# Two of twenty-five additions per step taken from TensorE and given to transfers in SBUF: products 0, 1 and 10, 11 added in pairs

## The reference

```python
x = x + deform(groupnorm(x))       # 32 groups of 8 channels

def deform(x):                     # DCNv4, 3 x 3 taps
    xdw = depthwise3x3(x) + dw_b
    om = xdw @ om_w + om_b         # per pixel and group: 9 taps x (dx, dy, mask)
    value = x @ vp_w + vp_b
    # every tap samples value bilinearly at its shifted place, times its mask
    out = sum_over_taps(mask * bilinear(value, tap + offset))
    return out @ op_w

x = x + binary_conv3x3(groupnorm(x)) * scale + bias     # second layer
```

## Time and profile before

| | us |
|---|---|
| median of 3 runs | 3860.18 (3853.02 to 3861.33) |
| the profiled execution's own time | 3859.76 |
| its span, first to last instruction | 3858.0 |
| PE busy over the span | 3628.5 (94%) |
| DVE busy | 3510.0 (91%) |
| ACT busy | 2286.0 (59%) |
| POOL busy | 565.0 (15%) |

### The profile page before, as it was taken

How to read it: one execution, slowest core, us unless ns; L and a number is a source line. 1 busy time by engine, 2 the same in 40 slices (tenths; PEclk the granted TensorE clock), 3 DMA queues, 4 the chain that set the end, 5 groups by cost and what they waited for, 6 DMA issues and landing times. The chain is left out here.

```text
span 3858.0 us, 90635 instructions
## 1 busy us (share of the span) xinstructions
PE 3628.5 (94%) x37696; PEld 2369.5 (61%) x37696; DVE 3510.0 (91%) x2757; ACT 2286.0 (59%) x4547; POOL 565.0 (15%) x412
## 2 busy tenths in 40 slices
PE   4899999999999999999999999999999999858998
PEld 2566666666666666666666666666666666623333
DVE  4899999999999999999999999989999999948776
ACT  5556665666666665666556666665566666235554
POOL 0011111101111111111111001111111111104444
PEclk9999999999999999999999999999999999979999
DMA  6454565445555555455545555555544554345563
GB/s 177 100 111 102 110 125 132 101 111 116 124 120 109 114 123 115 94 108 127 131 99 119 112 121 114 107 122 131 118 100 97 106 107 94 52 158 199 209 215 147
DMA packets 319939, 470.35 MB, mean 122 GB/s; under 512 B 37244, under 2 KB 242684, under 8 KB 313736
## 3 DMA queue, kind: packets, MB, share of 16 engines
q0 software_dynamic: 94080, 196.11, 28.4%
q1 hardware_dynamic: 224584, 266.07, 23.2%
q10 hardware_dynamic: 832, 2.10, 0.1%
HBM read 262.53 MB, written 67.41 MB: 86 GB/s over the span
## 5 line engine op out<-in xcount | busy, mean ns | idle before, releaser
L1026 DVE TENSOR_TENSOR pv<-val,wsum 128x2048 f32<-128x2048 f32 x800 | 1811.2, 2286 | 21.4 <-ACT xdw L557 14.6
L796 PEld LDWEIGHTS ps_add<-ident,pv 128*128 128x128 f32 x12800 | 1401.2, 142 | 356.0 <-issue 223.7
L796 PE MATMUL ps_add<-ident,pv 128*128 128x128 f32 x12800 | 1527.2, 275 | 70.9 <-DVE pv L1026 62.7
L751 PE MATMUL ps_om<-xdw,omw 128*32 128x256 f32 x13824 | 868.4, 384 | 30.4 <-ACT hat L587 29.4
L585 ACT ACTIVATE hat<-ps_om,omb 128x256 f32<-128x256 f32 x576 | 276.0, 479 | 551.2 <-PE ps_om L751 501.9
L979 DVE TENSOR_TENSOR prod<-hat,mwy 128x1536 f32<-128x1536 f32 (+1 forms) x384 | 526.0, 1397 | 82.9 <-DMA wsum<-prod 61.8
L472 POOL DMA_DIRECT2D wsum<-prod x192 | 226.0, 1254 | 2556.8 <-DVE wsum L979 2556.8
L751 PEld LDWEIGHTS ps_om<-xdw,omw 128*32 128x32 f32 x13824 | 391.2, 109 | 330.2 <-issue 95.5
L589 ACT ACTIVATE msk<-ps_om,omb 128x256 f32<-128x256 f32 x288 | 137.0, 476 | 401.4 <-PE ps_om L751 399.3
L965 DVE TENSOR_TENSOR mwy<-hat,msk 128x768 f32<-128x768 f32 x288 | 274.4, 953 | 94.3 <-ACT hat L599 94.3
L722 PE MATMUL ps_bg<-tri,diag 128*32 128x512 f32 x3024 | 346.5, 592 | 11.9 <-ACT tri L551 11.9
(11 more groups left out here) (134 smaller groups left out, 2622.7 us busy)
## 6 DMA issues: line engine op xcount, KB each, us to landing
wsum<-prod POOLq DMA_DIRECT2D x160, 768.0 KB, 7.1
tri<-in_x_dram SPq DMA_DIRECT2D x725, 128.0 KB, 2.9
win<-in_x_dram SPq DMA_DIRECT2D x144, 256.0 KB, 3.6
x<-xres SPq DMA_DIRECT2D x128, 256.0 KB, 5.1
xres<-in_x_dram POOLq DMA_DIRECT2D x124, 256.0 KB, 8.4
out_dram<-c_x SPq DMA_DIRECT2D x31, 1024.0 KB, 4.5
c_x<-x SPq DMA_DIRECT2D x30, 1024.0 KB, 5.3
c_box<-box_d SPq DMA_DIRECT2D x16, 1024.0 KB, 7.4
```

Of the source, the lines that this page charges most:

```text
L751: mm = nc.tensor.matmul(ps_om[G * q:G * q + G, (par + i) % 2, 0:TOK], omw[:, h, comp, :], xdw[:, j % 2, h, q, :], start=h == 0, stop=h == ...
L796: mm = nc.tensor.matmul(ps_add[:, tb, c, :], pv[:, (j + uv) % PBUF, c, P * tb:P * tb + P], consts["ident"][:, :], start=uv == 0 and c % 4 ...
L1026: nc.vector.tensor_tensor(pv[:, (j + uv) % PBUF, :, :].rearrange("p c (r w) -> p c r w", w=W), val[:, :, SR * j + u:SR * j + u + SR, v:v + ...
```

## The change

Products 0 and 1, and 10 and 11, are added in SBUF by a transfer from POOL's queue that reads the one buffer of `pv` and accumulates into the other (1 MB each), so that PE adds 23 instead of 25. PE adds 1 (which now holds 0 + 1) at the end of slot 5, and 11 (10 + 11) after the depthwise matmuls of slot 0. `pv` has five buffers instead of four. The room comes from `acc`, which now lies in `xres`, and from x ahead, whose two halves go through one buffer one after the other: the first is loaded after slot 7's sends and read by DVE at the end of slot 8, and only then the second is loaded, read in slot 1. ACT's copy of the sums into `acc` now waits for the stores of `xres`, which it did one slot later before. Code and numbers of what is left:

```diff
-PBUF = 4
+PBUF = 5
+PAIRED = {1: 0, 11: 10}
+PAIRS = list(PAIRED)
+ADDS_AT = [(13, 11, 14, 15), (16, 17, 18), (19, 20, 21), (22, 23, 24), (), (2, 3, 1), (4, 5, 6), (7, 8, 9), (12,)]
-        MEANS_AT = [1, 3]
-        SCALES_AT = [0, 2, 4, 6]
+        MEANS_AT = [2, 3]
+        SCALES_AT = [1, 2, 4, 6]
-        AHEAD_AT = 7
+        AHEAD_AT = 8
+                def add_pair(n, j, uv):
+                    s = STEPS * n + j
+                    pool.wait_ge(pv_full, SHIFTS * s + uv + 1)
+                    at_least(pool, pair_added, 16 * (len(PAIRS) * s + PAIRS.index(uv)))
+                    nc.gpsimd.dma_start(pv[:, (SHIFTS * j + uv) % PBUF, :, :], pv[:, (SHIFTS * j + PAIRED[uv]) % PBUF, :, :],
+                                        accum_op=ALU.add).then_inc(pair_added, 16)
...
                 def summed(s):
-                    act.wait_ge(add_done, SHIFTS * (s + 1))
+                    act.wait_ge(add_done, ADDS * (s + 1))
+                    at_least(act, x2_stored, 16 * Q * s)
...
                 def add(s, j, uv):
-                    pe.wait_ge(pv_full, SHIFTS * s + uv + 1)
-                    if uv == 0:
+                    if uv in PAIRED:
+                        pe.wait_ge(pair_added, 16 * (len(PAIRS) * s + PAIRS.index(uv) + 1))
+                    else:
+                        pe.wait_ge(pv_full, SHIFTS * s + uv + 1)
+                    if uv == ADDED[0]:
...
-                    def add_next(k, i):
-                        if k < SAMPLED and not first:
-                            add(s - 1, j - 1, SAMPLES_AT[k][i])
-                        elif k >= SAMPLED and i < len(SAMPLES_AT[k]):
-                            add(s, j, SAMPLES_AT[k][i])
+                    def add_next(k, early):
+                        before = [uv for uv in ADDS_AT[k][:1] if uv not in PAIRED]
+                        for uv in before if early else ADDS_AT[k][len(before):]:
...
-                    if not isinstance(s, int) or s > 0 or uv >= PBUF:
-                        dve.wait_ge(add_done, SHIFTS * s + uv - PBUF + 1)
+                    used, in_step = (uv - PBUF, s) if uv >= PBUF else (uv - PBUF + SHIFTS, s - 1)
+                    if used in PAIRED.values():
+                        dve.wait_ge(pair_added, 16 * (len(PAIRS) * in_step + list(PAIRED.values()).index(used) + 1))
+                    elif not isinstance(s, int) or in_step >= 0:
+                        dve.wait_ge(add_done, ADDS * in_step + ADDED.index(used) + 1)
```

More of the change, by code:

```diff
@@ L39 @@
 SAMPLED = 4
+PAIRED = {1: 0, 11: 10}
+PAIRS = list(PAIRED)
+ADDS_AT = [(13, 11, 14, 15), (16, 17, 18), (19, 20, 21), (22, 23, 24), (), (2, 3, 1), (4, 5, 6), (7, 8, 9), (12,)]
+ADDED = [uv for k in (4, 5, 6, 7, 8, 0, 1, 2, 3) for uv in ADDS_AT[k]]
+ADDS = len(ADDED)
 SENT_TAPS = (1, 2, 3, 6, 7)
@@ L95, in dw @@
         return only(first, "first", shares(FIRST_VALUES, u, DW_UNITS)) + only(not last, "dw", (u,))
-    return dw(0) + only(means, "mean", (0, 0)) + dw(1) + dw(2) + only(means, "mean", (1, 1)) + dw(3) + values(0) + only(not first, "back", range(4)) + values(1) \
+    return dw(0) + dw(1) + only(means, "mean", (0, 0)) + dw(2) + only(means, "mean", (1, 1)) + dw(3) + values(0) + only(not first, "back", range(4)) + values(1) \
         + only(not first, "project", range(4)) + values(2) + values(3)
@@ L217, in layer0 @@
         pv = sb("pv", [P, PBUF, GC, TOK])
-        acc = sb("acc", [P, TB, Q, GC, G])
         acc_t = sb("acc_t", [P, CH, Q * TOK])
-        ahead = [acc[:, :, :, :, :].rearrange("p b q c g -> p (b q c g)"),
-                 acc_t[:, :, :].rearrange("p h t -> p (h t)")]
+        ahead = acc_t[:, :, :].rearrange("p h t -> p (h t)")
         xres = sb("xres", [P, CH, Q, TOK])
+        acc = xres[:, :, :, :].rearrange("p h q t -> p (h q t)")\
+            .rearrange("p (b q c g) -> p b q c g", b=TB, q=Q, c=GC)
         tri = sb("tri", [P, CB, Q, SR, W])
@@ L454, in load_ahead @@
                         pool.wait_ge(bg_full, unit(n, j, "dw3", NI) + 1)
-                    nc.gpsimd.dma_start(ahead[half], src[:, HW // 2 * half:HW // 2 * (half + 1)]).then_inc(x_ahead[half], 16)
+                    if half == 1:
+                        pool.wait_ge(sums_made, CH * CH * n + CH * j + 1)
+                    nc.gpsimd.dma_start(ahead, src[:, HW // 2 * half:HW // 2 * (half + 1)]).then_inc(x_ahead[half], 16)
                 def add_residual(n, j, units):
@@ L836, in step @@
                             offsets(*ahead_of, 1)
-                        add_next(k, 0)
+                        add_next(k, True)
                         if ahead_of:
@@ L862, in _ @@
                 for k in range(SAMPLED):
-                    for uv in SAMPLES_AT[k]:
+                    for uv in ADDS_AT[k]:
                         add(STEPS * NI - 1, STEPS - 1, uv)
@@ L924, in sums_ahead @@
                     for i in range(HW // 1024):
-                        last = nc.vector.bn_stats(bs1[:, j, HW // 1024 * half + i, :], ahead[half][:, 512 * i:512 * i + 512])
+                        last = nc.vector.bn_stats(bs1[:, j, HW // 1024 * half + i, :], ahead[:, 512 * i:512 * i + 512])
                     last.then_inc(sums_made, 1)
@@ L1077, in step @@
                             mask_rows(*following(n, j), 0)
+                        if k == 1 and j in (1, 2) and has_next(n):
+                            sums_ahead(n, j - 1, 1)
+                        if k == SCALES_AT[0] and has_means(n, j, NI):
+                            dve.wait_ge(sums_made, CH * CH * (n + 1))
                         multiply_next(k, 2)
@@ L1096, in _ @@
                         multiply(NI - 1, STEPS - 1, uv)
-                statistics(NI - 1, STEPS - 2)
+                    if k == 0:
+                        statistics(NI - 1, STEPS - 2)
                 at = unit(NI - 1, STEPS - 1, "project3", NI) + 1 + BACK_UNITS
```

31 lines of the change are left out of this document (16 added, 15 removed).

## The result

| | before | changed |
|---|---|---|
| median of the runs, us | 3858.20 | 4041.18 |
| lowest to highest, us | 3853.02 to 3861.33 | 4037.93 to 4045.10 |
| ratio, 95% interval | | 1.0471 (1.0459 to 1.0484) |
| span of the profiled run, us | 3858.0 | 4038.9 |

Predicted were 3960 us and at most 4025. The direction and the mechanism hold; the loss is 183 us instead of 101.

A forecast was written before the change was run, and what follows sets the result against it. Neither PE nor DVE alone was taken as the bound. Per image, 17.2 us of new waits less 8.0 given back net 9.2, 74 us over 8 images; with 27 for the clock, 3960 us, range 3880 to 4025.

The forecast's parts named there:

- What bounds the kernel: Whole steps: neither PE nor DVE alone is the bound; less work on PE gives back at most 6.5 us per image.
- Rival A: PE's load counts and the order costs nothing, since PE reaches slot 8 late enough to find product 12: 3810 us, chance 0.11.
- Slot 8: PE's third component waits for product 12's addition and starts 5.1 us later, delaying ACT and slot 0's third component equally.
- Product 16: DVE waits for the buffer of 11, added late in slot 0: 3.7 us into step 3, 4.1 into step 0.
- the clock's price: PE's clock falls behind new pauses ahead of slot 0's third component: two per image at 1.7 us, 27 us in all.
- about 0.1 each: Product 16's wait into steps 1 and 2, where DVE does x ahead's statistics first and ACT has no edge to clear.
- rival C: PE's clock falls at nearly every new pause, five more per image, 68 us more: 4025 us, chance 0.12.
- Product 6: DVE waits for the addition of 1 at slot 5's end: 6.3 us in step 3, 2.6 in step 0.
- Given back: Per image, DVE regains 6.5 us of waits for weights and buffers, and about 1.5 of 8.0 us of transfer waits.
- Statistics and means moved by a slot: nothing added: DVE's statistics and means of x ahead, done a slot later, were taken to cost no time.
- The transfers of the pairs: Each 1 MB accumulation on POOL's queue takes 10 us, bounds 7.1 and some 16, hidden behind 12 us of cover.
- rival B: Pair transfers take 16 us instead of 10, so products 15 and 5 wait 3 to 4 us per step: 4050, chance 0.07.

The follow-up runs named there:

- fastest kernel: The changed kernel with product 12 added last in slot 8, product 10 made in slot 7, 15 and 18 a slot later, 1 added before 3: 3821.42 us.
- filled pauses: The changed kernel with matmuls of zeros on PE, 14 ahead of product 12's addition and 22 behind slot 0's addition of 13: 3986.53 us.
- later pair: The fastest kernel with the transfer of products 10 and 11 sent when product 12 is written, not when 11 is: 3825.95 us.

## Why the prediction missed, step by step

**What bounds the kernel: right in direction.** DVE's work did not shrink, and PE's saving became idle time. PE's busy time fell by 38.6 us and not by 120: 122 us of additions are gone, and I put the remaining 83 down to matmuls at the lower clock (durations such as 4.43 for 2.73). The fastest kernel bears this out: with the same 23 additions per step and a granted clock of 1.00 from 200 to 3200 us, its PE is busy 3510.6 us, 118 less than before. Rival A, by which the order costs nothing, is out: PE waits for product 12, by 2.9 to 6.2 us, in steps 0, 1 and 2 of each of images 1 to 6.

**Slot 8: the mechanism is shown.** Undoing this one place brings back 161 us. The term was 5.1 us of delay for the third component. In the rows it started 3.3 us ahead of DVE's cut before (1610.97 and 1614.23) and starts 3.4 behind it now (1694.76 and 1691.40): 6.6, of which 1.45 are the addition at half clock.

**Product 16: 8.0 + 3.4 predicted, 15.9 measured. The first step that failed is the clock's price.** The prediction priced two falls per image at 1.7 us each, and left slot 8's pauses to the range. The trace has 42 such pauses in images 1 to 6 (two at each seam into steps 1 to 3, one into step 0), and a fall behind 39 of them, 6.5 per image. By the rows above the first of a seam costs 1.45 us (3.42 for 1.97), the second 2.6 (4.43 for 2.73, and 1.93 for 1.07). With these two sizes the prediction's own count closes. Into step 3 it put product 16 at 18.9 us behind DVE's cut (1633.1 and 1614.2), and the row has 23.0 (1714.44 and 1691.40), later by 4.1, the two falls. Into step 0 it had a wait of 4.1; with one fall that is 6.7, and product 16 waits 6.6 and 6.8 in images 1 and 7, whose first step is not a turn of the loop. At the five turns it waits 1.7 to 2.1, behind 3.8 us in which DVE has already stood idle, and so the mean is 2.75. Into steps 1 and 2, "about 0.1 each" became 2.85 and 4.14. Into step 1 that is the clock: 0.15 is left where the filled pauses take the falls away. Into step 2 they leave the fall at slot 8 and 2.62, so how much of that is the clock stays open.

This is rival C, which I had given 0.12. C's whole clock term is 27 + 68 = 95 us; the filled pauses, which took away 22 of the 39 falls, returned 55.

**Product 6: 8.9 predicted, 5.1 measured** (by step 0.86, 0, 0, 4.25). PE's count from product 16 to product 6 was right: where product 6 waits, it starts 62.8 us behind product 16 in step 3 and 58.9 in step 0, against 63.2 and 59.5. DVE's count of 56.9 was too short, with 58.6 and 58.2 measured. It was read in one step of one image with 1.1 us of transfer waits in it, and the changed kernel has 2.7 and 2.4 there on the mean.

**Given back: the second step that failed.** Masks gave 4.0 of 6.5. The transfer waits were to fall by 1.5 per image and rose by 4.5. The fall came where it was forecast, behind product 16: slot 2's wait went from 1.5 to 0.2. The rise is in slot 8, from 1.7 to 7.4. What had covered the transfer there before were the mask waits of slot 7 (steps 0 and 3) and x ahead's statistics in slot 7 (steps 0 and 1). With both gone, slot 8 waits 1.8, 2.1, 2.4 and 1.2 us where before only step 2 waited 1.7. The kernel without pairs separates them: it keeps its mask waits, and besides step 2's 1.8 it waits in step 1 alone, 2.0 where there was nothing before. So "Statistics and means moved by a slot: nothing added" held for the time of that kernel (3858.90), but not once the mask waits were gone. That a wait given back is a gain needed a look at what is late next, and that was the transfer (7.1 us from issue to landing). Product 10 in slot 7, which covers it, takes 46 us off.

**The turn of the loop: not foreseen.** It is 3.2 us per image, though product 16's wait into step 0 is smaller behind it, and the later pair shows that taking it away need not give time.

**The transfers of the pairs: right.** The page's row of DMA issues, changed kernel (KB, us from issue to landing):

```profile
pv<-pv POOLq DMA_DIRECT2D x64, 1024.0 KB, 7.3
```

Taken were 10, with bounds of 7.1 and 16; DVE never waits for them, so rival B did not occur. The Trainium skill's fit for this path ("DMA: Bandwidth & Descriptors", "Anatomy of one DMA — SWDGE (gpsimd) path"), by which 1 MiB would be an estimated 4.4 us, is still too low, though by less than the row of 8.9 had it. That row was one of two of its size and queue in the trace before: the other one, which loads the other half of x ahead, has 5.2 (`acc<-in_x_dram`), nearer to the page, and the prediction did not weigh it.

**The sum.** Per image 12.6 predicted and 23.7 measured; the difference is product 16 +4.5, transfers +6.0, turn +3.0, masks +2.2, product 6 -3.8, rest -0.9. Times 8, the excess at product 16, which is the clock but for the open part in step 2, is 36 us and would by itself have stayed in the range (3996); the transfers are 48, the turn 24 and the masks 18, less 30 for product 6. So two steps failed: the clock, priced for two falls per image where there are 6.5, and the transfer waits, put at 1.5 less where they are 4.5 more. The whole of the clock cannot be had from the table, since its cost shows as waits at product 16. The range ended at 4025 because it took rival C alone and put the transfers, the turn and the masks at their forecast; they came together.

## What to carry to other kernels

Where an engine runs its instructions in program order, as PE does in these rows, ask of every one that you move whether its operand has landed by then and who waits for what stands behind it: here one addition, placed one item too early, cost 161 us. Here PE had 5% of slack, and work taken from it gave no time until the next-late thing, a transfer, was covered as well; neither measure alone gained, both together took 1% off. Before a wait is counted as given back, look at what it has been covering, and the same for any work that moves across a transfer.

## What the runs showed of the hardware

PE does not run a ready matmul past one whose data are missing: the third component starts at 1694.76, with the end of product 12's addition, though PE had stood idle for 5.71 us ahead of that addition. The Trainium skill ("TensorE: Matmul & The Clock Gate", "The mechanism") says that matmuls start and end in strict program order; these rows agree.

PE's granted clock fell behind short pauses. In images 1 to 6 of the kernel before, 4 of 12 pauses of 2.1 and 2.7 us were followed by a fall to the lower level; in the changed kernel 39 of 42 pauses of 2.8 to 6.2 us were, each for 3.4 to 6.8 us. Matmuls of zeros in part of the pauses took the falls from 39 to 17 and were worth 55 us.

An accumulation of 1 MB from SBUF into SBUF lands 7.3 us after its issue in the changed kernel (7.2 to 8.2 in the other runs), against 7.1 for 768 KB; in proportion to the size it would be 9.5.

At each of the five turns of the loop an instruction packet started only as a bulk transfer's packets ended (0.3 to 1.2 us ahead of the last; 1369.26 and 1369.6 at one turn), and DVE stood idle for 3.8 us. That the one holds up the other is argued from these times and from the idle time's absence when the transfer is later or missing; which resource they share stays open.
